# Values in one burst, experts in pairs of banks, and a float32 product for values and gates in an attention-and-experts kernel

## The reference

```
xn = layernorm(x)
q, k, v = xn Wq' + bq, xn Wk' + bk, xn Wv' + bv        (16 heads of 8 features)
attn    = softmax(causal(q k' / sqrt(8))) v Wo' + bo
logits  = xn gate_w'                                    (8 experts)
top_w   = softmax of the two largest logits
ffn     = sum over these two experts e of top_w * (xn We[e])
out     = x + attn + ffn
```

## Time and profile before

| | |
|---|---|
| time, median of three runs | 563.18 us (563.01 to 564.31) |
| profiled execution, its own time | 564.58 us |
| its span | 562.8 us |
| granted TensorE clock, mean | 0.993 |
| TensorE busy | 516.0 us (92% of the span) |
| VectorE busy | 439.1 us (78%) |
| ScalarE busy | 400.9 us (71%) |
| GpSimd busy | 346.4 us (62%) |

### The profile page before, as it was taken

The page is one execution under the profiler, slowest core; times in us unless marked ns, Lnnn a source line. Parts: engine busy times, 40 slices in busy tenths (PEclk is TensorE's granted clock), DMA queues, the critical chain, the costliest instruction groups (busy, mean ns, idle before and its releaser), DMA issues.

```text
span 562.8 us, 19500 instructions
## 1 busy us (share of the span) xinstructions
PE 516.0 (92%) x6402; PEld 402.3 (71%) x6402; DVE 439.1 (78%) x1109; ACT 400.9 (71%) x1033; POOL 346.4 (62%) x565
## 2 busy tenths in 40 slices
PE   1157999999999999999999999999999999999986
PEld 1145777777777777777777787777777778777754
DVE  3268888888888888888888888888888888877721
ACT  5624677777777777778777777777877777776664
POOL 4323576666666777666666677766666667754433
PEclk9999999999999999999999999999999999999988
DMA  3645555464455555544544555554445455540000
GB/s 98 172 98 139 137 138 137 110 145 125 110 132 137 145 137 135 134 130 120 128 128 117 137 145 136 131 139 126 128 118 133 115 139 147 137 130 12 12 12 20
DMA packets 64002, 67.11 MB, mean 119 GB/s; under 512 B 6752, under 2 KB 59104, under 8 KB 59104
## 3 DMA queue, kind: packets, MB, share of 16 engines
q1 hardware_dynamic: 63968, 66.68, 47.0%
HBM read 44.90 MB, written 21.23 MB: 118 GB/s over the span
## 4 chain that ended last, share of the span: by engine, by line
PE 79%; ACT 7%; DMA 4%; issue 4%; DVE 3%; POOL 2%; SPq 1%; ACTq 1%; POOLq 0%; DVEq 0%
PE m L779 26%; PE oT_ps L847 14%; PE scoreT_ps L823 10%; PE score_ps L803 9%; PE scoreT_ps L828 6%; PE score_ps L797 4%; ACT probs L473 3%; PE m L956 3%; DMA qstack<-mT 2%; PE m L951 2%; ACT parts L496 2%; PE m L893 1%; PE m L925 1%; DMA x_sb<-in_x 1%; PE m L914 1%
## 5 line engine op out<-in xcount | busy, mean ns | idle before, releaser
L589 DVE TENSOR_REDUCE negmax<-score_ps 128x2 f32<-128x512 f32 (+1 forms) x384 | 260.4, 686 | 51.9 <-PE score_ps L803 37.8
L473 ACT ACTIVATE probs<-scoreT_ps 128x512 f32<-128x512 f32 x384 | 225.8, 607 | 88.7 <-PE scoreT_ps L823 44.5
L779 PE MATMUL m<-we_hl,xnT_hl 128*128 128x512 f32 x384 | 122.9, 429 | 0.0
L847 PE MATMUL oT_ps<-probs,vaug 128*32 128x256 f32 (+1 forms) x2048 | 110.2, 333 | 0.0
L823 PE MATMUL scoreT_ps<-qstack,kstack 123*128 123x128 bf16 (+1 forms) x1024 | 102.7, 222 | 5.1 <-DMA qstack<-mT 4.5
L803 PE MATMUL score_ps<-kstack,qstack 72*128 72x128 bf16 (+1 forms) x1024 | 104.3, 224 | 1.9 <-DVE negmax L589 1.8
L372 POOL TENSOR_TENSOR fours<-lower,upper 128x512 f32<-128x512 f32 x64 | 81.8, 1278 | 22.1 <-ACT upper L508 21.3
L823 PEld LDWEIGHTS scoreT_ps<-qstack,kstack 123*128 123x128 bf16 (+1 forms) x1024 | 68.3, 98 | 33.1 <-issue 21.6
L366 POOL TENSOR_TENSOR parts<-rest,parts 128x256 bf16<-128x256 f32 x64 | 41.9, 673 | 72.0 <-ACT parts L501 71.6
L847 PEld LDWEIGHTS oT_ps<-probs,vaug 128*32 128x32 f32 x2048 | 53.6, 109 | 37.6 <-issue 5.4
L803 PEld LDWEIGHTS score_ps<-kstack,qstack 72*128 72x128 bf16 (+1 forms) x1024 | 71.1, 100 | 5.6 <-DVE negmax L589 3.8
(11 more groups left out here) (82 smaller groups left out, 696.6 us busy)
## 6 DMA issues: line engine op xcount, KB each, us to landing
kstack<-scratch SPq DMA_DIRECT2D x96, 192.0 KB
scratch<-parts SPq DMA_DIRECT2D x64, 192.0 KB, 2.4
qstack<-scratch SPq DMA_DIRECT2D x64, 192.0 KB
qstack<-scratch SPq DMA_DIRECT2D x32, 256.0 KB
x_sb<-in_x SPq DMA_DIRECT2D x32, 128.0 KB, 2.1
scratch<-parts SPq DMA_DIRECT2D x32, 128.0 KB, 1.9
out<-out_sb SPq DMA_DIRECT2D x32, 128.0 KB, 1.9
qstack<-mT SPq DMA_DIRECT2D x64, 8.0 KB, 1.8
```

Source lines behind the costliest of these rows:

```text
L473: a.activation(o, i, ACT.Exp, scale=SCALE).then_inc(act_exp, 1)
L589: v.tensor_reduce(o, score_ps[n % 2][:].rearrange("p (h k) -> p h k", h=w), axis=AX.X, op=ALU.max, negate=True).then_inc(dve_max, 1)
L779: ins = tn.matmul(o, l, r, start=i == 0, stop=i == len(products) - 1)
L847: ins = tn.matmul(o, va[:, q, h, :], i, start=q == 0 and grp % VGRP == 0, stop=q == 1 and grp % VGRP == VGRP - 1, skip_group_check=True)
```

## The change

It touches five things.
1. Values and gates become one float32 product for each row tile, with the weights `wvg_sb` as loaded. For it ScalarE copies the transposed input from `m1` into a new tile `xnT` (step 11), and VectorE's `halve_input` waits for that copy. The halves of the weights, their preparation and their semaphore steps go.
2. All four head groups of `values` run for sequence s-2 at step 5, behind that step's `scoreT_item`. `probs` has eight buffers for it, and ScalarE copies `oT` at step 6.
3. The expert banks run in pairs, lower and upper, at steps 3 and 8. ScalarE takes the upper ones at steps 4 and 9, VectorE the lower ones at 4 and 9.
4. The input transposes move from step 11 to step 10.
5. GpSimd's sums move from steps 1 and 10 to 0 and 9.

```diff
@@ GpSimd
-                    if n == (1 if has(s, -1) else 3) and has(s, -2):
+                    if n == 0 and has(s, -2):
                         sum_tile(t + (-2), 1)
...
-                    if n == 10 and has(s, -1):
+                    if n == 9 and has(s, -1):
                         sum_tile(t + (-1), 0)
@@ ScalarE
-                pr = probs[grp % 2]
+                pr = probs[f.c % 2 * NG + grp]
                 act.wait_ge(pe_scoreT, upto(f, per=ITEMS, k=k + 1))
                 if j == 0:
-                    if grp >= 2:
-                        act.wait_ge(pe_pv, upto(f, per=NG, k=grp - 1))
-                    else:
-                        act.wait_ge(pe_pv, upto(f + (-1), per=NG, k=NG + grp - 1))
+                    act.wait_ge(pe_pv, upto(f + (-2), per=NG, k=grp + 1))
...
-                    if n == 11 and has(s, -1):
-                        upper_experts(t + (-1), 1)
+                    if n == 11 and has(s, NXT):
+                        nxt = t + NXT
+                        act.wait_ge(pe_xnT, upto(nxt))
+                        a.copy(xnT[nxt.buf][:], m1[:, 0:S]).then_inc(act_xnT, 1)
                     f, k = behind(t, s, n)
                     if f:
                         take_exp(f, k)
...
-                    if n == 5 and has(s, -2):
+                    if n == 6 and has(s, -2):
                         fin = t + (-2)
                         act.wait_ge(pe_pv, upto(fin, per=NG))
                         act.wait_ge(pe_o, upto(fin + (-1)))
                         a.copy(oT[:].rearrange("p r t -> p (r t)"), oT_ps[:]).then_inc(act_oT, 1)
...
-                    if n == 6 and has(s, -1):
-                        upper_experts(t + (-1), 0)
+                    if n in (4, 9) and has(s, -1):
+                        upper_experts(t + (-1), 0 if n == 4 else 1)
@@ VectorE
             def halve_input(nxt, k):
                 if k == 0:
-                    dve.wait_ge(pe_xnT, upto(nxt))
+                    dve.wait_ge(act_xnT, upto(nxt))
...
-                    if n == 5 and has(s, -1):
+                    if n == 4 and has(s, -1):
                         lower_experts(t + (-1), 0)
@@ TensorE
-                    if n == 11 and has(s, NXT):
+                    if n == 10 and has(s, NXT):
                         pe.wait_ge(pool_xn, upto(t + NXT))
...
                         for q in range(QT):
-                            ins = by_halves(m1[:, q * VG:(q + 1) * VG], xnT_hl[t.buf][:, 0, q * P:(q + 1) * P],
-                                            xnT_hl[t.buf][:, 1, q * P:(q + 1) * P], wvg_hl[:, 0], wvg_hl[:, 1], whole=True)
+                            ins = tn.matmul(m1[:, q * VG:(q + 1) * VG], xnT[t.buf][:, q * P:(q + 1) * P], wvg_sb[:],
+                                            start=True, stop=True)
...
-                    if n == 3 and has(s, -2):
-                        values(fin, NG - 2)
-                    if n in (9, 11) and has(s, -1):
-                        values(mix, (n - 9) // 2)
                     if n in EXPERT_STEPS and has(s, -1):
-                        experts(mix, s, EXPERT_STEPS.index(n))
+                        q = EXPERT_STEPS.index(n)
+                        experts(mix, s, 2 * q)
+                        experts(mix, s, 2 * q + 1)
...
                     if n == 5 and has(s, -2):
-                        values(fin, NG - 1)
+                        for grp in range(NG):
+                            values(fin, grp)
...
-            EXPERT_STEPS = (4, 6, 8, 10)
+            EXPERT_STEPS = (3, 8)
```

More of the change, by code:

```diff
@@ L138, in bass_block @@
         wvg_sb = sb("wvg_sb", [P, VG])
-        wvg_hl = sb("wvg_hl", [P, 2, VG], FP32R)
         wo_sb = sb("wo_sb", [P, D])
@@ L155, in bass_block @@
         xb = sbs("xb", [P, QT, D])
+        xnT = sbs("xnT", [P, S])
         xnT_hl = sbs("xnT_hl", [P, 2, S], FP32R)
@@ L162, in bass_block @@
         weight = sbs("weight", [P, QT, E])
-        probs = sbs("probs", [P, 3, HG, P], n=2)
+        probs = sbs("probs", [P, 3, HG, P], n=2 * NG)
         stats = sb("stats", [P, QT, 6])
@@ L171, in bass_block @@
         w_high = sb("w_high", [P, E, D])
-        wvg_high = sb("wvg_high", [P, VG])
         parts = sb("parts", [P, 2, PARTS, S], BF16)
@@ L563, in between @@
                     act.wait_ge(dve_weights, 3)
-                    a.copy(wvg_hl[:, 0], wvg_high[:]).then_inc(act_weights, 1)
-                    act.wait_ge(dve_weights, 5)
                     a.copy(we_hl[:, 0], w_high[:]).then_inc(act_weights, 1)
@@ L762, in between @@
                     high_half(we_sb[:], w_high[:]).then_inc(dve_weights, 1)
-                    dve.wait_ge(dve_weights, 5)
+                    dve.wait_ge(dve_weights, 3)
                     low_half(we_sb[:], w_high[:], we_hl[:, 1]).then_inc(dve_weights, 1)
@@ L772, in _, with by_halves @@
             tn = nc.tensor
-            def by_halves(o, high, low, other_high, other_low, whole=False):
-                products = [(high, other_high), (high, other_low), (low, other_high)] + [(low, other_low)] * whole
-                for i, (l, r) in enumerate(products):
-                    ins = tn.matmul(o, l, r, start=i == 0, stop=i == len(products) - 1)
+            def by_halves(o, high, low, other_high, other_low):
+                for first, l, r in ((True, high, other_high), (False, high, other_low), (False, low, other_high)):
+                    ins = tn.matmul(o, l, r, start=first, stop=l is low)
                 return ins
@@ L838, in values @@
                     pe.wait_ge(act_oT, upto(f + (-1)))
-                pr, va = probs[grp % 2], vaug[f.buf]
+                pr, va = probs[f.c % 2 * NG + grp], vaug[f.buf]
                 c0 = S * (grp // VGRP)
@@ L869, in experts @@
                 if s == 1 and d == 0:
-                    pe.wait_ge(dve_weights, 6)
-                    pe.wait_ge(act_weights, 3)
+                    pe.wait_ge(dve_weights, 4)
+                    pe.wait_ge(act_weights, 2)
                 cols = slice(q * P, (q + 1) * P)
```

8 lines of the change are left out of this document (1 added, 7 removed).

## The result

The changed kernel takes 711.6 us (median of four runs, 710.8 to 712.3) against 563.1 for the kernel before, run beside it: a ratio of 1.263, interval 1.261 to 1.265. The forecast was 657 in 622 to 700, so the direction was right and the size was wrong, beyond the upper end. The profiled execution's own time is 711.03 us, 146.4 more than before's.

What follows compares the result with a forecast made beforehand. TensorE's own program, run end to end, was taken to bound each 15.62 us slot. Waits of 4.4 less gains of 1.15 gave 3.25 us a slot, 94 us with the edges: forecast 657 us, range 622 to 700.

Steps and rivals of the forecast that it cites:

- The clock: Rival: TensorE's idle share from wait 4 on halves its clock, about 1.6 us a fall; 680 us or over 700; chance 0.3.
- wait 4: Input transposes, now step 10: TensorE waits for VectorE's lower experts of row tile 1, 1.4 us a slot.
- The six waits: New TensorE waits for late helpers in each slot, adding to 4.4 us; rival of smaller waits, 3.3 us, chance 0.14.
- 1: Second expert bank of row tile 0, step 3: TensorE waits for VectorE to take the rests from m2, 0.75 us.
- 2: Last exponential before the scores of step 5, later because ScalarE gets the item behind the expert banks later: 0.1 us.
- 3: Attention output's transposes, step 7: TensorE waits for ScalarE's copy of oT, now at step 6, 0.9 us.
- 5: Output projection, step 11: TensorE waits for ScalarE's copy of oTn, as no values group stands between, 0.7 us.
- 6: Next slot's values and gates: TensorE waits for bank m1, held until VectorE's halves end behind the new copy, 0.55 us.
- (a): Values and gates as four float32 instructions instead of eight FP32R matmuls: 0.44 us a slot less.
- (b): Four groups of values in one burst save three entries and exits between matmul kinds: 0.6 us a slot less.
- (c): Expert banks in pairs save two changes of matmul kind, 0.05 each: 0.1 us a slot less.
- Float32 isn't cheaper: Rival: the float32 values-and-gates product needs as many passes as products; 14 us above forecast, 671 us; chance 0.05.

Runs made afterwards that it cites:

- e5: Changed kernel plus 90 empty semaphore increments in TensorE's idle start and 20 on ScalarE, shifting where the loops lie: 684.3 us (ratio 1.221).
- e3: e1 with five more matmuls of unread result ahead of the input transposes, where TensorE waits, in slots 4 and later: 676.8 us (1.202).
- e6: e5 with ScalarE's copy of oT ahead of step 6's exponential instead of behind it: 658.0 us (1.172).
- e9: e5 with both ScalarE's copy of oT ahead of step 6's exponential and the input transposes back at step 11: 617.6 us (1.098).
- b2f: b1f plus the four-group burst at step 5, oT and oTn copied ahead of exponentials, first expert bank and VectorE work re-placed: 597.5 us (1.068).
- e2: Kernel before plus 125 empty semaphore increments at the start of TensorE's program and 30 in ScalarE's: 604.2 us (1.074).
- b1g: b1f with ScalarE's three remaining key-buffer fills moved from between copy and cast to behind the projections' second part: 558.6 us (0.9946).
- b1f: Kernel before with the float32 values-and-gates product, both halves from the SBUF copy, first key-buffer fill ahead of the slots, loops aligned: 560.6 us (0.999).
- e1: Changed kernel plus 92 empty semaphore increments at TensorE's start and 201 on ScalarE, shifting where the loops lie: 690.4 us (1.225).

## Why the prediction was wrong

The 146.4 us of the two profiled executions, by the starts of the values-and-gates products. Up to slot 2: 73.19 against 66.83, 6.4. Slots 2 to 30: 592.1 against 454.2, 137.9. From slot 31 on: 2.2. Of the 137.9, the turns have 27.3 (e5), the other falls of the clock 13.6 (e3), and 27 x (19.05 - 15.62) = 92.6 are the plain slot's growth; slots 29 and 30 add 3.8. The sum is 145.9. The forecast had 94. Of the 52 more, the turns have 27.3, the clock 13.6, the slot's net 4.9, the start 4.9, and the end with slots 29 to 31 the rest.

- **The reload at the loop's turn** is the step that failed. The sum had no term for it and the rivals no case: the order of TensorE's blocks was argued, and where its code lies was not asked. The page of before has the two queues' packets, and its trace five turns without any. What the runs showed in its place: a reload of nine blocks at each of five turns, 27.3 us. Without it the kernel is at 684, inside the range.
- **The clock** was the rival at 0.3, with 680 for a fall in every second slot. Both it and the forecast's waits came, so it wasn't a case apart but a term. Its price, 1.6 us a fall, was a little high: the slots above show 20.27 - 19.05 = 1.2. It should have stood in the sum as well. The place was right: the filled wait 4 ended the loop's falls (e3), as did its removal (e4).
- **The six waits** were right, in helper, place and size. From start to start, less the block: 1, 0.80 (0.75 forecast); 2, 0.16 (0.1); 3, 0.86 (0.9); 4, 1.52 (1.4); 5, 0.73 (0.7); 6, 0.52 (0.55). Together 4.6 for 4.4. That one doesn't take away another, which the prediction had only argued, e6 and e9 show for waits 3 and 4. For the other four it rests on the sum: 4.6 less the gain is 3.5, and the slot grew by 3.43. What the prediction didn't see is that wait 4 itself covered 0.64 us for `o_sb`; that matters only to who removes it.
- **The gains**: (a) 0.37 for 0.44; (b) 3.52 - 2.84 = 0.68 for 0.6; (c) 0.05 for 0.1. Sum 1.10 for 1.15. The net is 3.5 worked out so, 3.43 measured, 3.25 forecast: 5 us over 27 slots. "Float32 isn't cheaper" fell. By the Trainium skill's four passes for true float32 (FP8 and Floating Point Precision, TensorE Precision Notes) nothing would have been gained here, 0.94 a block; the row has 0.57.
- **The edges** were mis-sized. The start got 1.5 for the new copy, and the copy alone does take 0.4. What it does to the program behind it, the fill that no longer lies beside TensorE's work, cost 3.6 more. The prediction looked for what hides a helper's work inside the slot, and not in `between`. The rest of the 6.4 is slots 0 and 1, with their own waits. The tail was 2.2 for 1.7.
- **"Nothing is hidden at the burst either"** held for the changed kernel, where VectorE stands idle 1.77 us under it; e9, with two waits cured, is still above before. That no placement could help is not shown: b2f halved the idle time, and lost 0.8 us or more to its slow low half.

Open: what sets the reload's length (2.7 to 3.9 us on TensorE at a turn, 6 us a turn in all in e2), and how much of the 27.3 is stall and how much cold clock. The issue rows carry 15.8 of it at the first item; the rest was not separated. b1g's slot 4 still comes 3.95 us later than before's, and which of the copy and the increments costs that was not tried. Nor was b2f with its halves read from bank `m1`.

## What to carry to other kernels

Where an engine runs its program without a gap, price an edit by both ends: what the block costs, and which helper the block had covered. One late helper can cost more than all that grouping saves (wait 4, 1.52 us, against 1.10), and the two such waits that were removed here added up. Where the core is a loop that nearly fills an engine's instruction memory, look at the instruction queues' packets before and after: here a shift by 125 cost 5% beside the padding itself, and 90 empty instructions in an idle stretch gave back 4%. Look at the program outside the loop with the same care: b1g differs from b1f by where three fills stand, and only b1g is faster than the kernel before. And when an operand moves from a matmul bank to SBUF, read the durations again: b2f's low half became three times as long.

## What the runs showed of the hardware

- A turn of the loop can be free or cost 6 us, by where the loop starts in TensorE's program: 563 to 604 us for the kernel before, shifted by 125 increments (11.4 of it the padding).
- ScalarE's reload is its own: in e2 the first queue has 65 packets and the second 15, and only TensorE has issue waits at the turns; in the changed kernel it is 64 and 40, and both have them.
- An empty semaphore increment holds TensorE 0.16 us (92 of them 15.0 us in e1, 125 of them 20.0 in e2): as padding it is free only beside idle time.
- 41 us at the half clock cost 13.6 us of time in this kernel (e1 against e3), less than the 20.5 that a TensorE at work throughout would lose by an estimate. Part of that time falls into its waits, which would explain it; that is argued.
- A subtraction on VectorE, 128x256, takes 0.42 us with one operand in a matmul bank, and 0.43 with both in SBUF; beside GpSimd's sum of two SBUF tensors the latter took 1.29 (b2f).
- Four float32 instructions of 136 columns take 0.57 us from start to start, eight FP32R ones of the same size 0.94.
